# Attention with relative position bias: the negated row maxima turned by two wide transposes a group and copied by four ScalarE operations, in place of eight narrow transposes and one copy

## The reference, cut to what matters

```
attn = jnp.einsum('bqd,bkd->bqk', q, k) / np.sqrt(HD)
attn = (attn.reshape(b * NH, h, w, h, w) + rel_bias_h[:, :, :, :, None] + rel_bias_w[:, :, :, None, :]).reshape(b * NH, hw, hw)
attn = jax.nn.softmax(attn, axis=-1)
out = jnp.einsum('bqk,bkd->bqd', attn, v)
```

## Time and profile before

| | us |
|---|---|
| median of three executions | 881.89 |
| lowest and highest | 879.38, 884.87 |
| the profiled execution, time | 880.72 |
| its span, first to last instruction | 878.9 |
| attention phase, from the first turn to its last copy out | 184.6 to 755.5 |
| busy over the span: PE, DVE, ACT, POOL | 775.8, 696.7, 574.0, 447.7 |

### The profile page before, as it was taken

One profiled execution on the slowest core, in us unless ns is written; L12 is line 12 of the kernel. 1 busy time (PEld: TensorE's weight loads), 2 busy tenths in 40 slices (PEclk: granted clock), 3 DMA queues, 4 the chain that ended last, 5 costly groups with the idle time before them and its releaser, 6 DMA issues. The chain is left out here.

```text
span 878.9 us, 14775 instructions
## 1 busy us (share of the span) xinstructions
PE 775.8 (88%) x5656; PEld 404.5 (46%) x5656; DVE 696.7 (79%) x965; ACT 574.0 (65%) x969; POOL 447.7 (51%) x284
## 2 busy tenths in 40 slices
PE   4999456588999999999999999999999998678874
PEld 2655456243444444444444444444444441356653
DVE  6998844696888888888888888888888880179995
ACT  1343335136787778787878777787777878257673
POOL 3677796445373738474665748373734444012120
PEclk9999767679999999999999999999999999889986
DMA  7675599999977584939293949577690001333411
GB/s 195 214 223 192 177 286 363 311 184 184 155 151 163 123 186 95 203 76 213 69 209 68 222 82 201 107 158 151 132 178 13 13 1 34 116 132 102 145 37 54
DMA packets 65750, 130.02 MB, mean 148 GB/s; under 512 B 9535, under 2 KB 45392, under 8 KB 57224
## 3 DMA queue, kind: packets, MB, share of 16 engines
q1 hardware_dynamic: 57648, 115.95, 57.1%
q10 hardware_dynamic: 8032, 13.13, 4.3%
HBM read 89.73 MB, written 34.60 MB: 141 GB/s over the span
## 5 line engine op out<-in xcount | busy, mean ns | idle before, releaser
L1031 DVE TENSOR_REDUCE at_neg_max<-at_r_ps 128x1 f16<-128x1024 f32 x384 | 451.7, 1218 | 86.4 <-PE at_r_ps L903 86.4
L989 ACT ACTIVATE at_probs<-at_s_ps 128x512 f32<-128x512 f32 x768 | 410.8, 600 | 97.4 <-PE at_s_ps L923 96.5
L923 PE MATMUL at_s_ps<-op_mix_q,op_mix_k 128*128 128x512 f16 x768 | 264.3, 383 | 10.8 <-issue 3.9
L903 PE MATMUL at_r_ps<-op_mix_k,op_mix_q 128*128 128x256 f16 (+1 forms) x1920 | 239.9, 258 | 13.3 <-DMA op_mix_q<-bias_parts 8.6
L935 PE MATMUL at_o_ps<-at_probs,op_v_u 128*32 128x512 f32 x1536 | 204.1, 604 | 0.0
L903 PEld LDWEIGHTS at_r_ps<-op_mix_k,op_mix_q 128*128 128x128 f16 x1920 | 157.3, 100 | 91.3 <-DVE at_neg_max L1031 15.7
L822 POOL COPY op_mix_q<-op_mix_q 2x4096 f16<-2x4096 f16 x48 | 171.6, 3601 | 1.5
L923 PEld LDWEIGHTS at_s_ps<-op_mix_q,op_mix_k 128*128 128x128 f16 x768 | 73.8, 97 | 175.5 <-issue 74.4
L220 POOL MEMSET op_mix_q<- 2x10240 f32 x12 | 103.5, 8628 | 21.2 <-PE at_o_ps L935 21.1
L826 POOL TENSOR_TENSOR at_o_sb<-at_o_sb,at_inv_rows 128x512 f32<-128x512 f32 x24 | 30.7, 1279 | 141.1 <-DVE at_inv_rows L1047 139.9
L819 POOL COPY op_mix_q<-op_mix_q 2x1024 f16<-2x1024 f16 x24 | 24.9, 1036 | 113.0 <-ACT op_mix_q L994 113.0
(11 more groups left out here) (116 smaller groups left out, 655.2 us busy)
## 6 DMA issues: line engine op xcount, KB each, us to landing
op_mix_q<-qk_parts SPq DMA_DIRECT2D x48, 640.0 KB, 10.7
op_mix_q<-bias_parts SPq DMA_DIRECT2D x120, 120.0 KB, 9.6
op_mix_q<-bias_parts SPq DMA_DIRECT2D x72, 128.0 KB, 9.5
qk_parts<-op_mix_q SPq DMA_DIRECT2D x24, 256.0 KB, 2.4
v_rows<-pr_v_st SPq DMA_DIRECT2D x8, 768.0 KB, 4.1
op_mix_k<-qk_parts SPq DMA_DIRECT2D x48, 128.0 KB, 13.2
op_v_u<-v_rows SPq DMA_DIRECT2D x12, 512.0 KB, 13.9
op_mix_q<-bias_parts SPq DMA_DIRECT2D x24, 256.0 KB, 9.9
```

What stands on the lines that cost most here:

```text
L903: last = pe.matmul(r_ps[count % RRING][:, first // GROUP, first % GROUP:first % GROUP + n], mix_q[owner.buf][:, variant, j, qt * P:(qt + 1 ...
L923: pe.matmul(s_ps[use % SRING][:, :], mix_k[unit.buf][:, j, keys], mix_q[unit.buf][:, ops.VARIANT_OF[kt], j, queries], start=True, stop=Tru ...
L989: act.activation(probs[n % PRING][:, j, :], s_ps[use % SRING][:, :], ACT.Exp).then_inc(s_taken, 1)
L1031: dve.tensor_reduce(neg_max[half][:, j // 2, t, j % 2:j % 2 + 1], r_ps[count % RRING][:, :, :].rearrange("p h t -> p (h t)"), AX_X, ALU.ma ...
```

## The change

`neg_max[half]` grows from two to 32 entries (`SLOT`) for each block of 128 queries; only the first two of each 32 are written by the reductions, and VectorE clears both tensors once ahead of the first reduction. The four blocks of a pair of heads then lie side by side as 128 columns, and one transpose turns them all: block t comes out at partition 32 t, two rows of it used. A half needs two transposes where it had eight, and the copy from PSUM becomes four ScalarE operations, one for each block, each of 2 x 256 elements, from partitions 0, 32, 64 and 96 to partition 96. The semaphore `s_taken` is raised by the last of the four.

```diff
-        neg_max = [ph.sb(f"neg_max{h}", [P, QUAD // 2, TILES, 2], F16) for h in range(2)]
+        neg_max = [ph.sb(f"neg_max{h}", [P, QUAD // 2, TILES, SLOT], F16) for h in range(2)]
...
         def max_rows(use):
-            return s_ps[use % SRING][:, :].bitcast(F16)[0:2, :].rearrange("p (g t) -> p g t", g=QUAD // 2)
+            return s_ps[use % SRING][:, 0:QUAD // 2 * P // 2].bitcast(F16).rearrange("p (g q) -> p g q", g=QUAD // 2)
...
                 for pair in range(QUAD // 2):
-                    for t in range(TILES):
-                        last = pe.transpose(max_rows(use)[:, pair, t * P:(t + 1) * P], neg_max[half][:, pair, t, :], ident16[:, :])
+                    last = pe.transpose(max_rows(use)[:, pair, :], neg_max[half][:, pair, :, :].rearrange("p t e -> p (t e)"), ident16[:, :])
                 last.then_inc(s_filled, 1)
...
-                act.activation(mix_q[unit.buf][MAX_ROW:MAX_ROW + 2, 0, 0::2, half * GROUP:(half + 1) * GROUP],
-                               max_rows(use), ACT.Copy).then_inc(s_taken, 1)
+                rows = mix_q[unit.buf][MAX_ROW:MAX_ROW + 2, 0, 0::2, half * GROUP:(half + 1) * GROUP]
+                for t in range(TILES):
+                    last = act.activation(rows[:, :, t * P:(t + 1) * P], max_rows(use)[t * SLOT:t * SLOT + 2, :, :], ACT.Copy)
+                last.then_inc(s_taken, 1)
...
+            for half in range(2):
+                dve.memset(neg_max[half][:, :, :, :], 0.0).then_inc(neg_cleared, 1)
+            dve.wait_ge(neg_cleared, 2)
```

More of the change, by code:

```diff
@@ L753, in phase_attention @@
         s_filled, s_taken, max_spread, pv_done = (ph.sem(n) for n in ("s_filled", "s_taken", "max_spread", "pv_done"))
-        row_scored, reduced = ph.sem("row_scored"), ph.sem("reduced")
+        row_scored, reduced, neg_cleared = ph.sem("row_scored"), ph.sem("reduced"), ph.sem("neg_cleared")
         o_out, sums_turned, inv_done, inv_spread, norm_done = (
```

## The result

The changed kernel takes 888.8 us in the median of 20 executions (883.79 to 895.66), against 882.69 us (876.91 to 888.62) of the kernel before in as many: a ratio of 1.0067, 95% interval 1.0047 to 1.0087. The ratio is an estimate from the single executions, not the quotient of the two medians, which would be 1.0069. The change is slower by 0.7%: 5.9 us by the ratio, 6.1 between the medians. The forecast was 889.7 us, 7.8 us or 0.9% slower. In the round of E1 to E4 one slow execution of the kernel before took 2594.26 us and counts in no ratio.

A forecast was written before the change was run, and what follows sets the result against it. TensorE, held each turn by transposes and then the copy, was taken as the bound. Copy starting 0.21 us earlier but lasting 1.56 against 1.01: +0.34 a turn, 23 turns 7.8; 881.9 + 7.8 = 889.7 us, range 883.5 to 893.0.

The forecast's parts named there:

- What bounds the turn: Attention turn: transposes until the copy can start, then the copy, lie in a row; one turn costs 0.71 us.
- The transposes: TensorE, each turn: two wide transposes start 1.00 us after weighing; scores j=0 come 0.30 earlier, the copy 0.21 earlier.
- the layout change: TensorE going from a 32-column strip to full width: about 0.1 us, now falling ahead of the wide transposes.
- The copies: ScalarE, each turn: four copies of 0.372 us, none overlapping, 1.56 us against 1.01; the turn grows by 0.34.
- How many turns: Attention: 23 of 24 turns count, 7.8 us; the first is lost in a later 3.90 us wait.
- Cover: GpSimd's copies have 3.7 us of cover; VectorE's reductions wait for TensorE, and its clears cost nothing.
- A: Rival: ScalarE's small copies overlap, four taking 1.18 us; 0.9 us faster, 881.0 us; chance 0.14.
- B: Rival: copies held, but TensorE pays no layout change ahead of wide transposes; 0.23 a turn, 887.2 us; chance 0.09.
- C: Rival: ScalarE's small copies have a larger fixed part; 0.39 us more a turn, 891.0 us; chance 0.18.
- D: Rival: the copy does not hold TensorE, whose saving arrives in full; 6.9 us faster, 875.0 us; chance 0.02.
- E: Rival: TensorE's longer standstill lowers its clock; over 30 us more, about 921 us; chance 0.02.

The follow-up runs named there:

- E1: Kernel before, narrow transposes kept, its copy cut into four of 2 x 256 elements that all read at partition 0: ratio 1.0033.
- E4: Kernel before's narrow transposes written block by block into four strips, with the changed kernel's four copies; against the kernel before, ratio 1.0047.
- E2: Changed kernel with its wide transposes, but one copy repeating block 0 for all four blocks; against the kernel before, ratio 0.9922.
- E3: Changed kernel with its wide transposes, but only block 0 copied; against the kernel before, ratio 0.9831.
- E7: Kernel before, narrow transposes with each pair in its own strip, ScalarE copying pair 0 and VectorE pair 1: 867.69 us, ratio 0.9847.
- E5: Changed kernel with its four copies shared, ScalarE taking blocks 0 and 1, VectorE 2 and 3; against the kernel before, ratio 0.9877.

## Why the prediction was right, point by point

**What bounds the turn.** The reading was that the transposes until the copy can start, and then the copy, lie in a row, and that TensorE's other work is short enough to wait. E2 shows the first link by itself (start 0.21 earlier, half period 0.21 less), E1 and the change the second, and E3 that TensorE alone is next. TensorE's standstill ahead of j=2 (the distance from j=1 to j=2 less 0.22) grew from 0.29 us to 0.92; the forecast had about 0.3 and about 0.9.

**The transposes.** First start 1.00 after the weighing (forecast 1.00), two of them 0.065 apart (0.06), scores j=0 earlier by 0.30 (0.30), copy earlier by 0.21 (0.21). E4 shows that the 0.1 us of the layout change is real and where it falls. The Trainium skill, TensorEngine Tiling (Array Packing), Key Properties, says that changing the tiling mode drains TensorE; these traces agree, as the wide weights are not loaded beneath the weighing as the narrow ones are, and put 0.1 us on it for this pair of layouts.

**The copies.** Each lasts 0.374 in the mean (forecast 0.372), and none overlaps. The working behind 0.372 had a flaw: L989's 600 ns and L540's 1.00 us don't give the slope of 0.833 ns for each element that it claims, but (1002 - 600) / 512 = 0.785. With that slope a copy would have been put at 0.41 and a turn at +0.49. The value was right all the same: single copies of 256, 512 and 1024 elements took 371, 585 and 1012 ns (E3, E7, before), which is 0.835 for each element and 158 fixed. The gap between the end of one and the start of the next is 0.01 us, not 0.024, which I had taken from the exponential behind L994. Four take 1.53, not 1.56. That is the only term of the sum that was off: a turn costs +0.31, not +0.34, and 23 of them 7.2 us instead of 7.8. The 7.2, a ratio of 1.008, lies inside the measured interval (1.0047 to 1.0087). That the time came within 0.9 us of the forecast is in part luck: the forecast started from 881.9, the median of three, where twenty executions give 882.69. The reason given, that a change of the group of 32 partitions read or written holds the operation behind, was an argument from one pair in the trace, beside a rule that the Trainium skill (VectorE: DVE Perf Modes, "Two Vector instructions with no wait between them") states for VectorE alone; E1 took away the changes of the group that is read, and the overlap came back. So the input side is shown, but for the stride, which changed with it. The output side is not: the exponential behind a copy writes in another group than the copy, but it also has 128 partitions where the copy has 2, and no run separates the two.

**How many turns.** 23 waiting turns stand in the list of waiters. Whether the first turn's delay is really lost behind the wait for the second unit's loads can't be read: the first copy out comes anywhere from 218.29 (E2) to 224.62 us (E7) in the nine traces, and a turn's 0.31 is lost in that.

**Cover.** VectorE's reductions, GpSimd's copies and the clears took nothing: E3's and E7's half periods come out within 0.02 us of sums that leave them out.

**The rivals.** A (overlap) is what E1 does (starts 0.27 apart, 1.16 in all, against 0.27 and 1.18), not the change. B would have needed transposes at 0.88; E4 shows what that takes. C, dearer small copies, fell with 0.374 us and starts 0.384 apart, where it needed 0.407. D, no wait for the copy, came only in E3 and E7, with copies of 0.37 and 0.58. It was priced too low: TensorE's saving of 0.30 a turn leaves out the 0.30 that the wait cost before, and E3 has 0.61 less. E, a lower clock, did not come: 1.00 as before.

## What to carry to other kernels

When a ring buffer ties two engines, price the whole chain from producer to the buffer's release: here TensorE saved 0.30 us a turn, but the copy started only 0.21 earlier and took 0.52 longer, so the turn became 0.31 dearer. Cutting one small ScalarE operation in four cost 0.17 us for each of the three further pieces, and 0.05 where they overlapped; here they overlapped only when all of them read in the same group of 32 partitions. Look for the split that lets pieces run side by side on the array and on two engines; the same transposes in two strips with one copy on each engine gave 1.5%.

## What the runs showed of the hardware that was not expected

VectorE copies two bytes to two bytes from PSUM faster than I had reckoned: 0.42 us for 2 x 512 elements (E7) where the expectation had 0.59, and 0.294 for 2 x 256 (E5). Small ScalarE copies that overlap are also shorter themselves: 354 ns in E1 for each that follows another, 371 for the first, against 374 in the change, for the same 256 elements. And the eight narrow transposes of f16, four at a time in strips, took 0.29 us from first start to last end, hardly more than the two wide ones (0.28).
